# Two graph attention layers: query products of the second layer two steps ahead and in front of the sums, edge products of the first layer three steps ahead

## The chip, the cores and the metric

The kernel runs on one core of one Trainium2 chip. The metric is the device time of one execution in microseconds. Three runs of the kernel before gave 5523.93, 5535.52 and 5536.22 us; their median is 5535.52 us.

## What is computed

Two graph layers, one after the other, over 6250 nodes and 200,000 edges sorted by target node. Each edge reads the row of its source node and the query of its target node, makes a score, and the scores of all edges of one target go through a softmax; the output of a node is the weighted sum of its edges' rows. Cut to what matters:

```
# layer 0 (4 heads of 32), e = projected edge attributes
kj    = k[src] + e
alpha = sum_c(q[dst] * kj) / sqrt(32)
a     = softmax of alpha over the edges of one dst
out   = segment_sum((v[src] + e) * a, dst)
# layer 1 (one head of 256)
s     = sum_c(q[dst] * k[src]) / 16 + edge_weight * we + be
a     = softmax of s over the edges of one dst
out   = segment_sum(v[src] * a, dst)
```

Around each edge stage there are small dense stages over the nodes (projections, a gate, layer norms, a feed-forward net), which the change doesn't touch.

## The kernel before

**Tiles, steps and chunks.** The edges are cut into tiles of 512 (4 groups of 128). A tile is paired with a window of 128 target nodes, 440 pairs in all; one pair is a *step*. Eight steps (st = 0 to 7) make a *chunk*; 55 chunks per layer. The same function edge(L) is written for each engine and run for L0 and for L1; chunks() calls its emit with `scores` (make the scores of chunk c) and `sums` (weigh and sum the messages of chunk c - 1), so each chunk scores its own edges while it sums the one before. There are 54 transitions between chunks with scores per layer.

**One step.** POOL issues four indirect DMAs (line 582), which gather 512 source rows of 1 KB into SBUF. It may run ahead: it waits only for the scores of the step five before (LEAD), for the landing of the gathers two steps before (`gathered`), and for a buffer that was freed long ago. SP loads for each pair the targets (`dst_row`, broadcast, 256 KB, line 431), the queries of the window (`qw`, 96 or 192.8 KB, line 433) and in layer 0 the edge attributes (`ea`, 128 KB, line 436), into four places; the load of pair g + 2 waits until the query products of pair g - 2 are counted on the semaphore `q`. A one-hot matrix `oht` (targets against nodes) is made by ACT in layer 0 (lines 668, 672) and by DVE in layer 1 (line 907).

**PE** (all its products have line 1291, the helper mm) makes for a step: in layer 0 the edge products edge_keys (ps<-w_c,ea, 4 matmuls) for DVE's line 916; the query products queries (ps<-qw,oht, 12 matmuls), which bring q[dst] to the edges; in layer 1 also bias_products (ps<-qw,oht with 3 columns, 4 matmuls), which give q times the key bias; and back (ps<-msg,oh or ps<-rows,oh, 4 matmuls), which sums the messages of a tile of the chunk before. PSUM has two buffers of each kind: edge_keys of pair g waits until DVE added those of g - 2 (semaphore `added`), queries of pair g until the scores of g - 2 are made (`score`), back until line 1089 took the sum two before (`acc`) and until the messages are weighed (`msg`).

**DVE** goes in a fixed order through a step. Layer 0: reduce the scores of the step before (line 928), multiply by the query products (line 923), add the edge products of the next step to its gathered rows (line 916), weigh messages (line 1064), accumulate sums (line 1089). Layer 1: dots, which multiplies and sums in one (line 939, four of them), the one-hot of the step after next (line 907), the weighed one-hots `oh` (line 1069), accumulate.

**The transition.** With the scores of a chunk complete, DVE masks them (line 989, semaphore `masked`) and PE transposes them (turn, lines 1370 and 1371). A scan over the edges for the maximum of each target follows in several pieces, which go to and fro between DVE and PE: scan_tiles (lines 999 to 1006), PE's arrange (ps<-spread,sel_h), scan_ends (lines 1012 to 1025), PE's carry_back (ps<-carry,sel_ht), scan_carried (lines 1030 to 1039), PE's turn_back (line 1385), subtract, PE's shrink_first. They lie in steps 0 and 1 of the next chunk, among that chunk's own products.

**What sets the order.** Each engine's order is written out by hand in emit, and an engine works its instructions in that order: a product that waits holds up all behind it. In PE's emit a step from 2 on is

```
if scores and more(c, st + 2):
    edge_keys(c, st + 2)
if scores and more(c, st + 1):
    queries(c, par, st + 1)
    if st + 1 < CH:
        bias_products(par, st + 1)
for r in L.summed[st] if sums and (L is L0 or st < CH - 1) else ():
    back(past, pp, r)
```

Of the kernel before, what the change touches and what calls it, by code (L numbers as in the profile page):

```python
# [31 lines left out]
CH = 8  # L32
# [34 lines left out]
def build(nc, a, out):  # L67
    ctx = ExitStack()
    with ctx:
# [1217 lines left out]
        def _(pe):  # L1287
# [39 lines left out]
            def edge(L):  # L1327
# [16 lines left out]
                def queries(c, par, st):  # L1344
                    c, st = c + st // CH, st % CH
                    g, b = CH * c + st, st % 2
                    after(pe, s["score"], g - 1)
                    queries_ready(c, st)
                    for j in range(JT):
                        for m in range(3):  # L1350
                            i = mm(q_ps(L, b)[:, j * L.D:(j + 1) * L.D], oht[st % PLACES][:, j * P:(j + 1) * P],
                                   qw[st % PLACES][:, m * L.QD:m * L.QD + L.D], m == 0, m == 2)
                    if L is L0 or st == 1:
                        i.then_inc(s["q"], 1)

                def bias_products(par, st):

                    if L is L1:
# [4 lines left out]
                        if st != 1:  # L1363
                            i.then_inc(s["q"], 1)
# [38 lines left out]
                def emit(c, par, scores, sums):  # L1403
                    past, pp = c - 1, 1 - par
                    if not sums:
                        edge_keys(c, 0)
                        edge_keys(c, 1)
                        queries(c, par, 0)
                    if sums:
                        turn(past)  # L1410

                    if scores:
                        bias_products(par, 0)
                    if L is L1 and sums and not (isinstance(past, int) and past == 0):
# [3 lines left out]
                    if scores and L is L1:  # L1418
                        queries_ready(c, 1)
                        bias_products(par, 1)  # L1420
                    if sums:
                        arrange(past)
                    if scores and L is L1:
                        queries(c, par, 1)
                    if sums:
                        carry_back(past)
                    if scores:
                        edge_keys(c, 2)
                        queries(c, par, 2)
                    if sums:  # L1430
                        turn_back(past)
                    if scores:
                        edge_keys(c, 3)
                    if sums:
                        shrink_first(past)
                    if scores:
                        bias_products(par, 2)
                    for st in range(2, CH):
                        if scores and more(c, st + 2):
                            edge_keys(c, st + 2)  # L1440
                        if scores and more(c, st + 1):
                            queries(c, par, st + 1)
                            if st + 1 < CH:
                                bias_products(par, st + 1)
# [143 lines left out]
```

## Time and profile before

| | |
|---|---|
| median of three runs | 5535.52 us (5523.93 to 5536.22) |
| the profiled execution | 5506.24 us |
| its span in the profile | 5504.4 us |
| PE busy | 3896.4 us (71%) |
| DVE busy | 4245.4 us (77%) |
| ACT busy | 1736.3 us (32%) |
| POOL busy | 3779.5 us (69%) |
| edge stage of layer 0, first to last gather | 147.5 to 2452.2 us |
| edge stage of layer 1, first to last gather | 2746.8 to 5115.5 us |
| mean granted clock of TensorE | 0.871 |

A row of the profile names the line, the engine, the operation and the tiles (written <- read). Busy time counts compute instructions; for POOL's gathers it is the time of the issuing instruction, while the transfer itself shows only in who waits for it. "Idle before" is the time that the engine stood still just before such instructions, with what ended it. "issue" there means that the profile shows nothing the engine waited for.

### The profile page before, as it was taken

The page shows a single profiled execution, that of the slowest core. Times are in us where ns is not written, and L with a number is a line of the kernel's source. Part 1 is how long each engine was busy: PE and PEld are TensorE (multiplying, and loading weights), DVE is VectorE, ACT ScalarE, POOL GpSimd, SP SyncE. Part 2 cuts the span into 40 slices and gives each one's busy share as a digit, 9 for nine tenths or more (in the row PEclk, how much of TensorE's full clock was granted, in tenths as well). Part 3 has the DMA queues.
Part 4 walks back from the last instruction along what each step waited for, and adds up shares of the span by engine and source line. Part 5 has one row for each costly group of instructions (what it writes and reads, how often), then busy time and mean ns, then how long its engine had stood idle before and what let it go on. Part 6 is the DMA issues. An engine that isn't in the chain of part 4 may idle for free.

```text
span 5504.4 us, 104662 instructions
## 1 busy us (share of the span) xinstructions
PE 3896.4 (71%) x26899; PEld 3265.3 (59%) x26899; DVE 4245.4 (77%) x14513; ACT 1736.3 (32%) x4325; POOL 3779.5 (69%) x4032
## 2 busy tenths in 40 slices
PE   7566666666666666666667777777777777777898
PEld 3556665656566665664445555555556656555687
DVE  7688778778877878776667777777777777777688
ACT  1466666666666666663300000000000000000132
POOL 0677777777777777762377777777777777777465
PEclk9788888888888888878978898988988888888899
DMA  6787878778888888763477777777777777777222
GB/s 178 201 216 210 208 207 217 206 208 212 216 214 205 214 213 213 209 171 108 119 196 202 196 200 197 197 201 200 200 195 200 202 200 204 198 194 199 78 81 67
DMA packets 777206, 1039.57 MB, mean 189 GB/s; under 512 B 206911, under 2 KB 528272, under 8 KB 776608
## 3 DMA queue, kind: packets, MB, share of 16 engines
q1 hardware_dynamic: 466736, 499.53, 35.0%
q0 software_dynamic: 169040, 436.01, 29.8%
q10 hardware_dynamic: 140832, 97.33, 5.7%
q8 instruction: 219, 3.59, 0.3%
q14 instruction: 379, 3.10, 0.2%
HBM read 929.76 MB, written 128.40 MB: 192 GB/s over the span
## 4 chain that ended last, share of the span: by engine, by line
POOL 28%; issue 28%; DMA 20%; DVE 10%; PE 9%; DVEq 2%; POOLq 1%; ACT 0%; ACTq 0%; SPq 0%
POOL rows L582 27%; DMA rows<-kv_d,idx 9%; PE ps L1291 9%; DMA rows<-x_d,idx 8%; DMA acc_d<-acc 2%; DVE prod L939 2%; DVE oh L1069 1%; DVE acc L1089 1%; DVEq L1145 1%; DVE oht L907 1%; POOL nq L605 1%; DVEq L1147 1%; DMA idx<-idx_d 1%; PE ps L1490 1%; POOLq L604 1%
## 5 line engine op out<-in xcount | busy, mean ns | idle before, releaser
L582 POOL DMA_INDIRECT rows<-kv_d,idx x1760 | 1713.4, 974 | 718.1 <-issue 524.2
L582 POOL DMA_INDIRECT rows<-x_d,idx x1760 | 1778.9, 1011 | 592.8 <-issue 517.7
L1291 PE MATMUL ps<-qw,oht 128*128 128x128 bf16 (+2 forms) x12320 | 1219.8, 252 | 27.1 <-DVE oht L907 26.9
L1291 PEld LDWEIGHTS ps<-qw,oht 128*128 128x128 bf16 x12320 | 1037.0, 106 | 229.3 <-issue 40.2
L1291 PE MATMUL ps<-rows,oh 128*128 128x257 f32 x3520 | 981.4, 433 | 209.9 <-DVE oh L1069 158.5
L939 DVE CUSTOM_DVE_ANT_0 prod<-rows,ps 128x256 f32<-128x256 f32 x1760 | 637.0, 418 | 413.4 <-DMA rows<-x_d,idx 307.6
L1291 PEld LDWEIGHTS ps<-rows,oh 128*128 128x128 f32 x3520 | 723.2, 214 | 339.1 <-DVE oh L1069 224.8
L916 DVE TENSOR_TENSOR rows<-rows,ps 128x1024 f32<-128x1024 f32 x440 | 536.0, 1218 | 355.7 <-DMA rows<-kv_d,idx 340.3
L1291 PE MATMUL ps<-msg,oh 128*128 128x132 f32 x3520 | 556.0, 309 | 347.7 <-DVE msg L1064 186.8
L708 ACT ACTIVATE pen_r<-ps 128x128 f32<-128x128 f32 (+1 forms) x110 | 30.0, 272 | 2188.0 <-PE ps L1371 2179.8
L1291 PEld LDWEIGHTS ps<-msg,oh 128*128 128x128 f32 x3520 | 484.1, 211 | 392.8 <-DVE msg L1064 374.6
L1291 PE MATMUL ps<-w_c,ea 128*128 128x128 f32 x3520 | 592.8, 323 | 30.4 <-DMA ea<-in_eaT 24.5
L1291 PEld LDWEIGHTS ps<-w_c,ea 128*128 128x128 f32 x3520 | 542.5, 235 | 40.1 <-issue 23.7
L678 ACT ACTIVATE oh<-iota_row,rel 128x128 f32<-128x128 f32 x1760 | 542.0, 386 | 33.3 <-PE ps L1291 32.0
L1069 DVE TENSOR_SCALAR oh<-iota_row,rel,prob 128x128 f32<-128x128 f32 x1760 | 489.9, 362 | 1.1 <-issue 0.7
L668 ACT ACTIVATE oht<-dst_row,node_tab 128x512 bf16<-128x512 int32 x440 | 312.0, 710 | 147.5 <-DMA dst_row<-in_dst_row 115.4
L1089 DVE SCALAR_TENSOR_TENSOR acc<-acc,keep_tab,ps 128x132 f32<-128x132 f32 (+1 forms) x770 | 317.6, 412 | 49.1 <-issue 26.2
L928 DVE TENSOR_REDUCE score<-prod 128x16 f32<-128x512 f32 x440 | 301.8, 686 | 44.7 <-issue 11.1
L672 ACT ACTIVATE oht<-oht,ones 128x512 bf16<-128x512 bf16 x440 | 311.4, 720 | 27.2 <-issue 1.1
L923 DVE TENSOR_TENSOR prod<-rows,ps 128x512 f32<-128x512 f32 x440 | 298.6, 679 | 15.6 <-PE ps L1291 7.6
L1064 DVE TENSOR_TENSOR msg<-rows,prob 128x512 f32<-128x512 f32 x440 | 292.4, 685 | 0.9 <-issue 0.6
L595 POOL TENSOR_TENSOR rows<-rows,minus_half 128x1 f32<-128x1 f32 x196 | 106.4, 558 | 252.9 <-DVE rows L1166 252.9
(205 smaller groups left out, 4341.2 us busy)
## 6 DMA issues: line engine op xcount, KB each, us to landing
dst_row<-in_dst_row SPq DMA_DIRECT2D x880, 256.0 KB
qw<-q_d SPq DMA_DIRECT2D x440, 192.8 KB
acc_d<-acc ACTq DMA_DIRECT2D x440, 128.5 KB
ea<-in_eaT SPq DMA_DIRECT2D x440, 128.0 KB
qw<-q_d SPq DMA_DIRECT2D x440, 96.0 KB
acc_d<-acc ACTq DMA_DIRECT2D x440, 66.0 KB
rows<-kv_d,idx POOLq DMA_INDIRECT x1760
rows<-x_d,idx POOLq DMA_INDIRECT x1760
```

Source lines behind the costliest of these rows:

```text
L582: pool.indirect_dma_start(out=L.rows[par][:, st, j, 0:D], out_offset=None, in_=L.table, in_offset=bass.IndirectOffsetOnAxis(ap=idx[par][:, ...
L668: act.activation(oht[st % PLACES][:, :], dst_row[st % PLACES][:, :], ACT.Abs, scale=-1.0, bias=node_tab[:, bass.ds(g, 1)])
L672: act.activation(oht[st % PLACES][:, :], oht[st % PLACES][:, :], ACT.Relu, scale=-1.0, bias=ones[:, 0:1])\
L678: act.activation(oh[:, st % OHS, j, :], iota_row[:, :], ACT.Abs, scale=-1.0, bias=rel[par][:, st, j:j + 1])
L916: v.tensor_tensor(kv, kv, e_ps(b).rearrange("p (j n) -> p j n", j=JT).unsqueeze(2) .to_broadcast([P, JT, 2, DM]), ALU.add).then_inc(s["add ...
L923: v.tensor_tensor(half, kv_rows[par][:, st, :, 0:DM], q_ps(L, st % 2).rearrange("p (j n) -> p j n", j=JT), ALU.mult)
L928: v.tensor_reduce(score[par][:, st * JT:(st + 1) * JT, :], prod[:, :, st % 2 * DM:(st % 2 + 1) * DM] .rearrange("p j (h n) -> p j h n", h= ...
L939: i = v.tensor_tensor_reduce(out=prod[:, j, :], in0=x1_rows[par][:, st, j, 0:D], in1=q_ps(L, b)[:, j * D:(j + 1) * D], scale=1.0, scalar=0 ...
L1064: v.tensor_tensor(m, kv_rows[par][:, st, :, DM:2 * DM].rearrange("p j (h c) -> p j h c", h=HEADS), prob[par][:, st * JT:(st + 1) * JT, :]. ...
L1069: i = v.tensor_scalar(oh[:, st % OHS, j, :], iota_row[:, :], rel[par][:, st, j:j + 1], prob[par][:, st * JT + j, 0:1], ALU.is_equal, ALU.mult)
L1089: v.scalar_tensor_tensor(acc[st % ACCS][:, 0:L.AW], old[:, 0:L.AW], keep_tab[:, bass.ds(g, 1)], agg_ps(L, b), ALU.mult, ALU.add).then_inc( ...
L1291: return pe.matmul(out_, lhsT=lhsT, rhs=rhs, start=first, stop=last)
```

## The change

Only PE's instructions move; DVE, ACT, POOL and SP keep theirs.

- Layer 1: queries of step st + 2, no longer of st + 1, are made in step st. So the products of steps 0 and 1 of a chunk are made in steps 6 and 7 of the chunk before, those of step 2 stand in the transition where those of step 1 stood, those of step 3 in front of turn_back.
- Layer 1: the bias products of steps 0 and 1 both stand right behind turn, those of steps 2 and 3 both behind shrink_first. The count on `q` now always comes with a step's bias products; before, step 1's came with its query products.
- Layer 0: edge_keys of step st + 3, no longer of st + 2, are made in step st, and stand behind the queries, no longer in front of them. In the transition edge_keys of steps 3 and 4 stand where those of 2 and 3 stood.

```diff
-                    if L is L0 or st == 1:
+                    if L is L0:
                         i.then_inc(s["q"], 1)
...
-                        if st != 1:
-                            i.then_inc(s["q"], 1)
+                        i.then_inc(s["q"], 1)
...
                         queries(c, par, 0)
+                        if L is L1:
+                            queries(c, par, 1)
                     if sums:
                         turn(past)
-
                     if scores:
                         bias_products(par, 0)
+                        bias_products(par, 1)
                     if L is L1 and sums and not (isinstance(past, int) and past == 0):
                         back(past - 1, par, CH - 1)
                     if scores and L is L0:
                         queries(c, par, 1)
-                    if scores and L is L1:
-                        queries_ready(c, 1)
-                        bias_products(par, 1)
+                        if not sums:
+                            edge_keys(c, 2)
                     if sums:
                         arrange(past)
                     if scores and L is L1:
-                        queries(c, par, 1)
+                        queries(c, par, 2)
                     if sums:
                         carry_back(past)
                     if scores:
-                        edge_keys(c, 2)
-                        queries(c, par, 2)
+                        edge_keys(c, 3)
+                        queries(c, par, 2 if L is L0 else 3)
                     if sums:
                         turn_back(past)
                     if scores:
-                        edge_keys(c, 3)
+                        edge_keys(c, 4)
                     if sums:
                         shrink_first(past)
                     if scores:
                         bias_products(par, 2)
+                        bias_products(par, 3)
                     for st in range(2, CH):
-                        if scores and more(c, st + 2):
-                            edge_keys(c, st + 2)
-                        if scores and more(c, st + 1):
-                            queries(c, par, st + 1)
-                            if st + 1 < CH:
-                                bias_products(par, st + 1)
+                        ahead = st + (1 if L is L0 else 2)
+                        if scores and more(c, ahead):
+                            queries(c, par, ahead)
+                            if ahead < CH:
+                                bias_products(par, ahead)
+                        if scores and more(c, st + 3):
+                            edge_keys(c, st + 3)
```

On PE at the transition between two chunks of layer 0 there stood before, from step 6 on (the numbers behind ea, qw and oht are the place, which is the step modulo 4; lines 1370 and 1371 are turn, ps<-msg,oh is back, carry is carry_back):

```order
L1291 MATMUL ps<-w_c,ea0 128x128 x4
L1291 MATMUL ps<-qw3,oht3 128x128 x12
L1291 MATMUL ps<-msg,oh 128x132 x4
L1291 MATMUL ps<-w_c,ea1 128x128 x4
L1291 MATMUL ps<-qw0,oht0 128x128 x12
L1291 MATMUL ps<-msg,oh 128x132 x4
L1370 MATMUL ps<-ident,biased 128x128
L1371 MATMUL ps<-ident,pen 128x128
L1291 MATMUL ps<-qw1,oht1 128x128 x12
L1291 MATMUL ps<-spread,sel_h4 4x128
L1291 MATMUL ps<-carry,sel_ht4 128x64
L1291 MATMUL ps<-w_c,ea2 128x128 x4
```

and after the change, from step 6 on too (turn has lines 1369 and 1370):

```order
L1291 MATMUL ps<-qw3,oht3 128x128 x12
L1291 MATMUL ps<-w_c,ea1 128x128 x4
L1291 MATMUL ps<-msg,oh 128x132 x4
L1291 MATMUL ps<-qw0,oht0 128x128 x12
L1291 MATMUL ps<-w_c,ea2 128x128 x4
L1291 MATMUL ps<-msg,oh 128x132 x4
L1369 MATMUL ps<-ident,biased 128x128
L1370 MATMUL ps<-ident,pen 128x128
L1291 MATMUL ps<-qw1,oht1 128x128 x12
L1291 MATMUL ps<-spread,sel_h4 4x128
L1291 MATMUL ps<-carry,sel_ht4 128x64
L1291 MATMUL ps<-w_c,ea3 128x128 x4
```

The edge products that read ea2, those of step 2 of the new chunk, moved from behind carry_back to a place ahead of the last back and of turn.

On PE at the transition of layer 1 there stood before, from step 6 on (128x256 are the query products, 128x3 the bias products, ps<-rows0,oh is back):

```order
L1291 MATMUL ps<-rows0,oh 128x257 x8
L1291 MATMUL ps<-qw0,oht0 128x256 x12
L1370 MATMUL ps<-ident,biased 32x128
L1371 MATMUL ps<-ident,pen 32x128
L1291 MATMUL ps<-qw0,oht0 128x3 x4
L1291 MATMUL ps<-rows0,oh 128x257 x4
L1291 MATMUL ps<-qw1,oht1 128x3 x4
L1291 MATMUL ps<-spread,sel_h1 1x128
L1291 MATMUL ps<-qw1,oht1 128x256 x12
L1291 MATMUL ps<-carry,sel_ht1 32x64
L1291 MATMUL ps<-qw2,oht2 128x256 x12
L1385 MATMUL ps<-ident,full 128x32
```

and after the change:

```order
L1291 MATMUL ps<-rows1,oh 128x257 x8
L1291 MATMUL ps<-qw1,oht1 128x256 x12
L1369 MATMUL ps<-ident,biased 32x128
L1370 MATMUL ps<-ident,pen 32x128
L1291 MATMUL ps<-qw0,oht0 128x3 x4
L1291 MATMUL ps<-qw1,oht1 128x3 x4
L1291 MATMUL ps<-rows1,oh 128x257 x4
L1291 MATMUL ps<-spread,sel_h1 1x128
L1291 MATMUL ps<-qw2,oht2 128x256 x12
L1291 MATMUL ps<-carry,sel_ht1 32x64
L1291 MATMUL ps<-qw3,oht3 128x256 x12
L1384 MATMUL ps<-ident,full 128x32
```

As many products stand between turn and turn_back as before, but each is of the next step, and the bias products of step 1, which are now counted on `q`, stand right behind those of step 0.

## Rows read from the trace of the kernel before

**Rows 1.** The page: busy time, and the chain by engine and line
```profile
PE 3896.4 (71%) x26899; PEld 3265.3 (59%) x26899; DVE 4245.4 (77%) x14513; ACT 1736.3 (32%) x4325; POOL 3779.5 (69%) x4032
POOL 28%; issue 28%; DMA 20%; DVE 10%; PE 9%; DVEq 2%; POOLq 1%; ACT 0%; ACTq 0%; SPq 0%
```
**Rows 2.** The gathers' line: ns min/median/max, first and last start; then all idle before them
```profile
L582 POOL DMA_INDIRECT rows<-kv_d,idx x1760: 940/946/1630, 147.5 to 2452.2; - x196
L582 POOL DMA_INDIRECT rows<-x_d,idx x1760: 992/998/1257, 2746.8 to 5115.5; - x196
...
L582 POOL DMA_INDIRECT rows<-kv_d,idx x1760 | 1713.4, 974 | 718.1 <-issue 524.2
L582 POOL DMA_INDIRECT rows<-x_d,idx x1760 | 1778.9, 1011 | 592.8 <-issue 517.7
```
**Rows 3.** Timeline, POOL's longest waits of layer 1, four in a row
```profile
3586.72 1.09 POOL L582 DMA_INDIRECT rows<-x_d,idx  x1 [2.38 <-issue]
3753.78 1.00 POOL L582 DMA_INDIRECT rows<-x_d,idx  x1 [3.54 <-issue]
3920.94 0.99 POOL L582 DMA_INDIRECT rows<-x_d,idx  x1 [1.86 <-issue]
4089.41 1.00 POOL L582 DMA_INDIRECT rows<-x_d,idx  x1 [4.04 <-issue]
```
**Rows 4.** Who waited for whom in 200 to 2462 us: total us, times, longest
```profile
DVE rows L916 <- DMA rows<-kv_d,idx: 327.0, 208, 5.3
POOL rows L582 <- DMA rows<-kv_d,idx: 59.8, 109, 2.1
POOL rows L582 <- DVE score L928: 6.1, 20, 0.3
DVE prod L923 <- PE ps L1291: 4.8, 9, 0.8
```
**Rows 5.** The same view in 2796 to 5122 us
```profile
DVE prod L939 <- DMA rows<-x_d,idx: 280.7, 201, 6.2
DVE prod L939 <- PE ps L1291: 72.4, 79, 2.2
POOL rows L582 <- DMA rows<-x_d,idx: 38.6, 94, 1.5
POOL rows L582 <- DVE score L939: 8.8, 29, 0.3
```
**Rows 6.** Timeline of a layer 0 transition, PE and DVE: start, us, row, idle before
```profile
2246.05 1.05 PE L1291 MATMUL ps<-w_c,ea 128*128 128x128 f32 x8
2247.61 1.12 PE L1291 MATMUL ps<-msg,oh 128*128 128x132 f32 x8
2248.65 1.22 DVE L916 TENSOR_TENSOR rows<-rows,ps 128x1024 f32<-128x1024 f32 x1
2250.34 0.33 PE L1370 MATMUL ps<-ident,biased 128*128 128x128 f32 x1 [1.61 <-DVEq L990]
2255.75 1.22 DVE L916 TENSOR_TENSOR rows<-rows,ps 128x1024 f32<-128x1024 f32 x1 [2.81 <-DMA rows<-kv_d,idx]
```
**Rows 7.** Timeline of a layer 1 transition: turn, carry_back, turn_back and SP's target loads
```profile
3054.35 0.40 PE L1370 MATMUL ps<-ident,biased 128*32 128x128 f32 x1 [4.11 <-DVEq L990]
3055.87 0.33 SPq L431 DMA_DIRECT2D dst_row<-in_dst_row  x1
3061.21 1.49 PE L1291 MATMUL ps<-qw,oht 128*128 128x256 bf16 x12
3061.83 0.33 SPq L431 DMA_DIRECT2D dst_row<-in_dst_row  x1
3064.63 0.24 PE L1385 MATMUL ps<-ident,full 32*128 32x32 f32 x1 [1.93 <-DVEq L1039]
```
**Rows 8.** Stretches of that transition: PE, PEld, DVE, ACT, POOL, clock, DMA share, GB/s
```profile
3060.00:3063.00 3.00, 2.70 (x24) 1.89 (x21) 2.54 (x15) 0.00 (x0) 2.38 (x3) 1.00 0.92 277
```

## The prediction

> **What bounds the kernel now.** I read the page first, for busy shares. No engine is near full: DVE has 77%, PE 71%, POOL 69%, and the chain that ended last names POOL and "issue" for 56% [rows 1]. That pair made me look at POOL's line. The reader should see there that POOL is not idle for 31% of the time in any useful sense. A gather's instruction takes 0.946 us in layer 0 and 0.998 in layer 1 in the median [rows 2], and between two of them lie 0.30 us in which POOL waits for nothing that shows. So 1760 gathers need at least 1760 x 1.246 = 2193 us in layer 0 and 1760 x 1.298 = 2284 us in layer 1. The stages take, from first gather to the end of the last, 2305.7 and 2369.7 us [rows 2]. POOL's own pace fills 95% and 96% of them, and the two stages are 85% of the span. Nothing that PE does shortens that pace.
>
> What is left over is 2305.7 - 2193 = 113 us and 2369.7 - 2284 = 86 us. A part is longer gather instructions: 1713.4 - 1760 x 0.946 = 48 us and 1778.9 - 1760 x 0.998 = 22 us [rows 2]. The rest, some 64 us in each layer, is waiting. I asked what POOL waited for. Its longest waits come every 167 to 168 us [rows 3], which is 128 gathers at 1.30 us; they follow POOL's count of instructions and are no one's fault on PE. Then there are waits for the landing of the gathers two steps before: 59.8 us in 109 times in layer 0 and 38.6 us in 94 times in layer 1 [rows 4, 5]. Of each the usual 0.30 us would pass anyway, which leaves 27 and 10 us. Never did POOL wait for DVE's scores: the rows that name them have 0.3 us as their longest [rows 4, 5], the usual gap. DVE, in turn, waited for gathers for 327.0 us in layer 0 and 280.7 us in layer 1 [rows 4, 5], that is 6.0 and 5.2 us per chunk (by 54 of them). So the order is: POOL's pace, then landings, then DVE with slack, then PE behind DVE.
>
> **The change part by part.** It adds and takes away no instruction; it moves PE's products.
>
> *Layer 1, query products two steps ahead.* They were late for DVE: line 939 waited for PE for 72.4 us in 79 times [rows 5], mostly in the steps 0 to 2 of a chunk. Those 72.4 us should go nearly to zero, since the products of steps 0 and 1 are now made while the old chunk runs out. But DVE then comes earlier to a gather that hasn't landed, and the 280.7 us grow by as much. Cover: POOL's pace. Worth on the path: 0. The products put in front of turn run while PE stood idle 4.11 us before turn [rows 7], and take 1.49 us [rows 7], so turn isn't late.
>
> *Layer 1, step 3's products in front of turn_back.* The 12 matmuls begin when DVE has made the scores of step 1, and PE stood idle for 1.93 us before turn_back [rows 7]. I take 0.3 us of delay of the scan per transition, 54 x 0.3 = 16 us on DVE, between 0 (the idle time holds them) and 1.49 us (it doesn't). DVE's 5.2 us of waiting for gathers per chunk hide either. Worth: 0.
>
> *Layer 0, edge products behind the queries and one step earlier.* In steps 2 to 6 they fill the time in which PE waits for DVE to weigh messages, and DVE needs nothing of PE there (4.8 us in all [rows 4]). Worth: 0. In step 7 the move costs something. The edge products of the new chunk's step 2 may start only when DVE has added those of step 0, and DVE does that after its last work for the old chunk. The last back and turn now queue behind that. In the timeline DVE's add begins at 2248.65 and ends at 2249.87; the edge products take 1.05 us, back 1.12 us, so turn can start at 2252.04 instead of 2250.34 [rows 6]. With back's sum and the transposed scores both later, DVE's scan begins some 1.7 us later: 54 x 1.7 = 92 us on DVE. What covers it is seen in the same rows: DVE reaches the add of the next step and waits 2.81 us for the gather. Over the layer it is 6.0 us of such waiting per chunk against 1.7. And if a chunk has less, POOL doesn't ask for a score until five steps later. Worth: 0; without the cover, 92 us.
>
> *Loads.* SP's four places are freed by the count on `q`, so moving it moves DMAs, and this is the one way in which PE touches POOL. In layer 1 the count for steps 0 and 1 now comes at once, behind turn. Before, SP loaded at 3055.87 behind turn and again at 3061.83, 6 us apart [rows 7]; now the second load (256 + 192.8 KB) follows the first within some 1.5 us. The counts of steps 2 and 3 come together too, and the counts of steps 4 to 7 a step earlier, so before turn there is a longer stretch with no loads. At the rate of this transition, 277 GB/s [rows 8], 449 KB are 1.6 us. A gather in flight then lands up to 1.6 us later and one that used to meet the second load lands earlier. The change in all lies between 0 - 10 us (all waits of layer 1 for landings go) and 54 x 1.6 = 86 us (none of the delay is hidden). Landing ended POOL's wait in 94 of 440 steps, and cost 10 us in them, so the lower end is the nearer. For two of eight steps getting worse and one better I take +3 us. In layer 0 the load that is tied to step 1's queries was issued later than its count anyway, and the rest moves by about one edge product: 0, within +-10 us of landing waits.
>
> Here a rule bears on the load term. The Trainium skill, page "DMA: Bandwidth & Descriptors", section "Queues, rings and completion order", says that each DMA engine takes turns between queues packet by packet; by it a second load in SP's queue stands behind the first and not ahead of the gather, and the sum would stay at 0. The same section says that a semaphore increment lands only after earlier writes of that DMA engine on all queues, which speaks the other way, for a late landing. No row of the kernel before tells which weighs more.
>
> Sum on the profiled execution: 5506 + 0 + 0 + 0 + 3 = 5509 us. The median of the runs is 29 us above that execution, so I forecast 5538 us, no change that can be measured. About 0.3%, 17 us, is what a measurement of this kernel can tell from no change.
>
> **The rivals.**
>
> *A. Bunched loads make POOL wait (slower).* At each transition of layer 1 the two loads, and the stores of sums that ACT issues behind turn, meet the gather of step 1, and POOL's gather of step 3 waits for its landing. It decides when landings of step 1 come later than POOL's next step allows in most chunks rather than in one of five. For: landings already end one of five waits, and the DMA share is 0.92 there [rows 8]. Against: the bytes are the same, and the stretch before has fewer loads. Price: 54 x 1.6 us x 0.4 (between the one in five of today and the half) = +35 us: 5570. Chance 0.20.
>
> *B. The late turn of layer 0 shows (slower).* If DVE were paced by its scan and not by gathers, 92 us would come through: 5628. Against it stand 6.0 us of waiting per chunk. Chance 0.04.
>
> *C. Landing waits shrink (faster).* In layer 1 loads are asked for a step earlier through most of the chunk and in both layers PE asks sooner, so fewer loads fall beside a gather that POOL is about to need. It can win at most the 27 + 10 us of landing waits and what long gather instructions cost through contention; I price it at two thirds of 37 us, -25: 5510. Chance 0.14.
>
> *D. DVE was the pace after all (faster).* Then the 72.4 us that line 939 waited for PE come off: 5463. The chain does spend 19% on DVE and PE [rows 1]. Against: DVE never ended a wait of POOL, and the waits of DVE for gathers are four times as long. Chance 0.04.
>
> *That the change doesn't do what it says* can be left out for layer 1: the order rows show the products moved. For layer 0 it is half true: in steps 2 to 6 the edge products only change places with the sums and the queries, since DVE's add, which lets them start, lies where it lay.
>
> **How the numbers follow.** No change (A to D absent) has 0.58. Faster by over 0.3% is C and D, 0.18; slower is A and B, 0.24. The range goes from 5505 (C, a little over its price) to 5580 (A, with a part of the 86 us bound); outside lie B, D and the far ends of A and C, in all under 2 in 10.
>
> **What would show it.** In the profile after: the first and last gather of both layers within some 10 us of their old distance; gathers' medians 0.95 and 1.00 us; no POOL wait for scores above 0.3 us. Line 939's wait for PE in layer 1 should fall from 72.4 us to under 15, and its wait for gathers rise from 280.7 to about 340. In layer 0 the wait of line 916 for gathers should fall from 327.0 by 50 to 92 us, to 235 to 280, as turn is some 1.7 us later. SP's two loads behind turn should be 1 to 2 us apart. POOL's wait for landings in layer 1 decides between the forecast (up to 45 us) and A (70 us and more). I am wrong if the gather stages shorten or lengthen by over 17 us together: then landings or DVE hold POOL in a way that I read as covered.

## The result and the profile after

The changed kernel takes 5578.08 us in the median of four runs (5575.36 to 5592.18), the kernel before 5533.41 us (5523.93 to 5536.22). The ratio is 1.0089, with a 95% interval of 1.0068 to 1.011: slower by 0.9%, 45 us. The forecast was no change, 5538 us. The profiled execution of the kernel before was 27 us faster than its median and that of the changed one 14 us slower than its own, so the two traces are 86 us apart where the medians are 45 us apart. To keep this out, the changed kernel was run again (e5_changed), and readings are checked against that second trace.

The gathers' own line in the changed kernel: ns min/median/max, and first and last start. Its first and last starts answer to the upper rows of [rows 2].

```profile
L582 POOL DMA_INDIRECT rows<-kv_d,idx x1760: 940/946/1698, 148.0 to 2467.8; - x196
...
L582 POOL DMA_INDIRECT rows<-x_d,idx x1760: 992/998/1257, 2774.5 to 5199.7; - x196
```

The pace of a gather is untouched: 946 and 998 ns. From the first to the last start layer 1's gathers took 2368.7 us before and now take 2425.2 us, 56 us more. Layer 0's went from 2304.7 to 2319.8 us, 15 us more; but in e6_l1_only and e18_l1_only_held below, whose layer 0 is that of the kernel before, it is 2324.9 and 2321.0 us, so these 15 us are not the change's: the trace of the kernel before was short there.

What POOL and DVE waited for in layer 1 of the changed kernel, in 2824 to 5208 us (total us, times, longest), against [rows 5]:

```profile
PE ps L1291 <- DVE oht L907: 501.1, 296, 4.8
DVE prod L939 <- DMA rows<-x_d,idx: 286.9, 181, 4.7
POOL rows L582 <- DMA rows<-x_d,idx: 76.8, 88, 3.1
DVE prod L939 <- PE ps L1291: 43.4, 52, 1.0
POOL rows L582 <- PE ps L1291: 23.9, 45, 1.5
POOL rows L582 <- DVE score L939: 12.8, 42, 0.3
```

POOL's wait for landings has doubled, from 38.6 to 76.8 us, in fewer cases, so each is longer. It still never waits for a score: 0.3 us is the longest. DVE waits less for PE (72.4 to 43.4 us, and none over 1.0 us), which is what the change was to do, and as long for gathers as before. PE has now a wait that it hardly had (26.9 us in the whole span before): its products, a step further ahead, wait 501.1 us for one-hots that DVE has not made yet. That costs nothing on this kind of chip, as e7_l1_held below shows. The row that puts 23.9 us of POOL's waits down to PE needs care: POOL waits for several semaphores at once, the sums of PE among them are those of two chunks before, and 12 of its 15 waits of over 0.6 us stand at step 1, where landings are late (below).

The same view for layer 0, 200 to 2478 us, against [rows 4]:

```profile
PE ps L1291 <- DMA ea<-in_eaT: 273.0, 54, 7.0
DVE acc L1089 <- PE ps L1291: 257.8, 55, 6.6
DVE rows L916 <- DMA rows<-kv_d,idx: 73.2, 149, 3.9
POOL rows L582 <- DMA rows<-kv_d,idx: 58.2, 106, 2.1
POOL rows L582 <- DVE score L928: 18.6, 61, 0.3
```

Once in each of 54 transitions PE waits some 5 us for `ea`. DVE's wait for gathers has shrunk from 327.0 to 73.2 us. POOL's is what it was (59.8 to 58.2 us).

One transition of layer 0 in the changed kernel, PE, DVE and SP's loads of `ea`, against [rows 6]:

```profile
2263.36 0.33 SPq L418 DMA_DIRECT2D idx_d<-idx  x1
2265.56 0.48 SPq L436 DMA_DIRECT2D ea<-in_eaT  x1
2267.87 0.47 SPq L436 DMA_DIRECT2D ea<-in_eaT  x1
2267.98 1.22 DVE L916 TENSOR_TENSOR rows<-rows,ps 128x1024 f32<-128x1024 f32 x1
2270.86 2.05 PE L1291 MATMUL ps<-w_c,ea 128*128 128x128 f32 x8 [4.41 <-DMA ea<-in_eaT]
2272.70 1.97 PE L1291 MATMUL ps<-msg,oh 128*128 128x132 f32 x8
2274.46 0.42 PE L1369 MATMUL ps<-ident,biased 128*128 128x128 f32 x1
```

DVE's add ends at 2269.20, but the edge products that stand before back and turn begin at 2270.86, because their `ea` has not landed: SP issues that load only behind keep_idx (line 418, at 2263.36), which waits until DVE has marked the chunk's edges with their owners (line 976). Then they run at half the pace of [rows 6], 2.05 us against 1.05, after the long stop (the clock is in the last section). Turn is at 2274.46, 5.3 us after the add ended; in [rows 6] it was 0.5 us.

And one transition of layer 1 in the changed kernel (turn, SP's loads of targets, ACT's stores, POOL):

```profile
4101.56 0.30 PE L1369 MATMUL ps<-ident,biased 128*32 128x128 f32 x1 [1.85 <-DVEq L990]
4102.06 4.85 ACTq L694 DMA_DIRECT2D acc_d<-acc  x3
4102.11 1.01 POOL L582 DMA_INDIRECT rows<-x_d,idx  x1 [0.30 <-issue]
4102.87 0.33 SPq L431 DMA_DIRECT2D dst_row<-in_dst_row  x1
4105.36 0.34 SPq L431 DMA_DIRECT2D dst_row<-in_dst_row  x1
4111.25 1.00 POOL L582 DMA_INDIRECT rows<-x_d,idx  x1 [0.30 <-issue]
4114.28 1.00 POOL L582 DMA_INDIRECT rows<-x_d,idx  x1 [2.04 <-DMA rows<-x_d,idx]
```

The two loads come at 4102.87 and 4105.36, 2.5 us apart and no longer 6 us [rows 7]. POOL issues the gathers of step 2 from 4102.11 on, right among them and ACT's three stores. Its first gather of step 4, at 4114.28, waits 2.04 us for them to land. The prediction's rival A had named the gather of step 1 and the wait at step 3; it is step 2 and step 4.

### The profile page after: what moved, and what is told of

Same layout as the page of the kernel before. It is cut to its first block, busy times and chain, and to the rows that moved or that the text cites. A ratio compares the mean times of both kernels' runs of the same rounds, so it can differ in the third digit from the quotient of the medians.

```text
span 5590.3 us, 104607 instructions
## 1 busy us (share of the span) xinstructions
PE 3998.9 (72%) x26899; PEld 3287.0 (59%) x26899; DVE 4256.0 (76%) x14513; ACT 1722.8 (31%) x4325; POOL 3790.7 (68%) x4032
## 3 DMA queue, kind: packets, MB, share of 16 engines
q0 software_dynamic: 169040, 436.01, 30.3%
## 4 chain that ended last, share of the span: by engine, by line
issue 26%; POOL 24%; DMA 23%; PE 11%; DVE 9%; DVEq 2%; ACT 2%; POOLq 1%; ACTq 1%; SPq 0%
POOL rows L582 23%; DMA rows<-x_d,idx 12%; PE ps L1291 10%; DMA rows<-kv_d,idx 8%; DMA acc_d<-acc 2%; DVE rows L916 1%; DVE prod L939 1%; DMA ea<-in_eaT 1%; ACT oh L678 1%; POOL nq L605 1%; DVE acc L1089 1%; DVEq L1147 1%; PE ps L1492 1%; DVE oht L907 1%; POOLq L604 1%
## 5 line engine op out<-in xcount | busy, mean ns | idle before, releaser
L1291 PE MATMUL ps<-qw,oht 128*128 128x128 bf16 (+2 forms) x12320 | 1273.8, 259 | 545.7 <-DVE oht L907 531.6
L1291 PEld LDWEIGHTS ps<-qw,oht 128*128 128x128 bf16 x12320 | 1016.7, 107 | 806.7 <-DVE score L939 602.8
L1291 PE MATMUL ps<-w_c,ea 128*128 128x128 f32 x3520 | 650.7, 342 | 512.4 <-DMA ea<-in_eaT 303.1
L1291 PE MATMUL ps<-rows,oh 128*128 128x257 f32 x3520 | 934.9, 417 | 2.4 <-DVE oh L1069 2.3
L1291 PEld LDWEIGHTS ps<-w_c,ea 128*128 128x128 f32 x3520 | 555.9, 241 | 582.9 <-issue 293.7
L1291 PEld LDWEIGHTS ps<-rows,oh 128*128 128x128 f32 x3520 | 707.8, 209 | 109.1 <-DVE oh L1069 3.3
L1291 PE MATMUL ps<-msg,oh 128*128 128x132 f32 x3520 | 521.2, 302 | 8.8 <-DVE msg L1064 4.7
```

The source lines that it names most:

```text
L1291: return pe.matmul(out_, lhsT=lhsT, rhs=rhs, start=first, stop=last)
```

## The experiments

Each kernel was timed in five rounds beside the kernel before on the same chip; the ratio is to that. The chips are of two kinds. On two draws the kernel before took 5533.38 and 5520.90 us, as in the first measurement (below: *chips of kind 1*); on three it took 7033.54, 6955.53 and 6956.38 us (*kind 2*). A ratio is good for its own kind of chip only; one chip of kind 2 was drawn twice and gave 7033.54 and then 6955.53 us, so times are compared within a set. The changed kernel as it is ran on kind 1 only, e10_scores_held and e11_before_held, with their repetitions, on kind 2 only.

| run | kernel | median us | kernel before | ratio, 95% interval |
|---|---|---|---|---|
| e1_l1_only | layer 1's part | 6988.44 | 7033.54 | 0.9936 (0.9916 to 0.9956) |
| e2_l0_only | layer 0's part | 7164.74 | 7033.54 | 1.0179 (1.0158 to 1.0199) |
| e3_border | changed, border of layer 0 restored | 7014.43 | 7033.54 | 0.9975 (0.9959 to 0.9992) |
| e4_l1_held | changed, all loads of layer 1 held | 7190.68 | 7033.54 | 1.0196 (1.0167 to 1.0224) |
| e5_changed | changed | 5584.16 | 5533.38 | 1.0093 (1.008 to 1.0106) |
| e6_l1_only | layer 1's part | 5573.06 | 5533.38 | 1.0072 (1.0059 to 1.0085) |
| e7_l1_held | changed, all loads of layer 1 held | 5524.32 | 5533.38 | 0.9984 (0.9973 to 0.9996) |
| e8_border | as e3_border | 5580.64 | 5533.38 | 1.0081 (1.0064 to 1.0098) |
| e9_second_held | changed, second load held | 7027.57 | 6955.53 | 1.011 (1.0079 to 1.014) |
| e10_scores_held | changed, loads held by scores | 7009.07 | 6955.53 | 1.0077 (1.0054 to 1.01) |
| e11_before_held | before, all loads held | 6938.55 | 6955.53 | 0.9974 (0.996 to 0.9987) |
| e12_l1_only_held | layer 1's part, all loads held | 6924.6 | 6955.53 | 0.9956 (0.9939 to 0.9974) |
| e13_second_held | as e9 | 7034.05 | 6956.38 | 1.0106 (1.0082 to 1.0129) |
| e14_scores_held | as e10 | 7016.7 | 6956.38 | 1.0078 (1.0059 to 1.0098) |
| e15_before_held | as e11 | 6953.18 | 6956.38 | 0.9989 (0.9968 to 1.0009) |
| e16_l1_only_held | as e12 | 6932.28 | 6956.38 | 0.9959 (0.9944 to 0.9975) |
| e17_second_held | as e9 | 5541.2 | 5520.9 | 1.0035 (1.0024 to 1.0046) |
| e18_l1_only_held | as e12 | 5517.54 | 5520.9 | 0.9989 (0.9977 to 1.0002) |

**First set, a chip of kind 2.** e1_l1_only takes layer 0's edits back, e2_l0_only layer 1's. In e3_border only the border is taken back:

```diff
                         queries(c, par, 1)
-                        if not sums:
-                            edge_keys(c, 2)
+                        edge_keys(c, 2)
...
-                        if scores and more(c, st + 3):
+                        if scores and st != CH - 1 and more(c, st + 3):
                             edge_keys(c, st + 3)
```

e4_l1_held leaves PE alone and edits SP in load_ahead:

```diff
                     wait(s["q"], g - 1)
+                    if L is L1:
+                        wait(s["score"], g - 2)
+                        if st == 3:
+                            wait(s["spreadback"], c)
                     load_pair(
```

> The change in layer 1 alone; layer 0 keeps its order of before. Theory (two separate costs: in layer 0 the edge products of the next chunk's step 2 wait for the load of ea and hold back and turn; in layer 1 the loads of targets and queries fall at other times and gathers land later): slower than before by 20 to 50 us, POOL's stage of layer 1 (2746.8 to 5115.5 us before, 2774.5 to 5199.7 in the changed kernel) longer by 20 to 56 us, layer 0 as before (line 916's wait for gathers about 327 us). Rival (the whole loss is layer 0's, and layer 1's longer stage in the one profile is chance): within 10 us of before. Rival (layer 1's part is a gain that layer 0 eats): faster than before by 10 us or more.

> The change in layer 0 alone; layer 1 keeps its order of before. Theory: slower than before by 10 to 30 us: PE waits some 5 us per transition for ea (273.0 us in 54 times in the changed kernel), line 916's wait for gathers falls to about 75 us, POOL's stage of layer 0 grows by some 15 us and the way from its last gather to layer 1's first by some 12 us. Rival (all of layer 0's delay is covered by POOL's pace): within 10 us of before.

> The changed kernel, but in layer 0 the edge products of the next chunk's step 2 stand behind queries of step 1, and no longer in front of the last back and of turn; all else as changed. Theory: PE's wait for ea before turn goes (273 us to under 60), turn comes 4 to 6 us earlier against POOL's steps, line 916's wait for gathers goes back above 250 us, and the kernel is 10 to 30 us faster than the changed one. Rival (layer 0 costs nothing): as slow as the changed kernel, within 8 us.

> The changed kernel, with PE's order untouched, but in layer 1 SP holds each load of a pair until the scores of the step three before the loading step's pair are made, and the second load behind turn until carry_back, so about when they came before the change. Theory (load times make gathers land late in layer 1): 15 to 50 us faster than the changed kernel, POOL's wait for landings in layer 1 from 76.8 us back to about 40. Rival (it is PE's order itself: products in front of the sums make sums and so DVE late): no faster than the changed kernel, landings' wait still above 65 us.

Measured: layer 1's part alone is faster by 0.6%, layer 0's alone slower by 1.8%, with the border restored the change is faster by 0.25%, and with layer 1's loads held it is slower by 2.0%. That layer 1's part would be a gain was one of e1's rivals; layer 0's loss is 131 us where 10 to 30 were expected, and holding the loads brought nothing that was hoped for. This chip is bound elsewhere. The waits of e2_l0_only over the whole span:

```profile
PE ps L1291 <- issue: 803.0, 728, 7.3
POOL rows L582 <- DVE score L928: 944.2, 197, 9.1
POOL rows L582 <- DVE score L939: 635.9, 180, 9.4
```

Here PE stands still for 803 us with nothing in the profile that it waits for, up to 7.3 us at a time, and POOL waits for DVE's scores for 1580 us, up to 9.4 us at a time. The gathers' instructions take what they took. So POOL no longer sets the pace; it follows DVE's scores, and what delays PE and DVE can reach the time: layer 0's part costs 1.8%, query products made earlier gain 0.6%. Nearly all of layer 0's loss is the border: from first to last start its gathers take 3129.6 us in e1_l1_only (layer 0 as before), 3278.8 us in e2_l0_only and 3144.3 us in e3_border. It is not the load of `ea` there (7.1 us of waiting in 200 to 3436 us of e2_l0_only), but DVE's add, for which PE's products wait 429.5 us in 119 times. Why PE stops on such a chip isn't shown by any run.

**Second set, a chip of kind 1.** e7_l1_held is e4_l1_held with the same waits written on one line.

> The changed kernel itself, beside the kernel before on the same chip, since another chip ran the kernel before in 7033.54 us and not in 5533. If this chip is like the first: slower than before by 0.7 to 1.1%. If it is like the second, where layer 0's part alone cost 1.8% and layer 1's alone gained 0.6%: slower by 1.0 to 1.4%, the two parts added.

> Layer 1's part alone, as e1_l1_only, on this chip. On a chip like the first: slower than before by 0.2 to 0.9% if load times in layer 1 make gathers land late (POOL's wait for landings in layer 1 near 77 us); within 0.2% of before if the first chip's loss was all layer 0's. On a chip like the second: faster by 0.4 to 0.9%, because DVE there doesn't wait for gathers and query products made earlier are of use.

> The changed kernel with layer 1's loads held as in e4_l1_held. On a chip like the first: 0.2 to 0.8% faster than the changed kernel if load times are the cost in layer 1, no faster if PE's order is. On a chip like the second: slower than the changed kernel by some 0.8%, since there the loads are late already.

> The changed kernel with layer 0's edge products of the next step 2 moved back behind queries of step 1, as e3_border. On a chip like the first: 0.2 to 0.5% faster than the changed kernel, PE's wait for ea in layer 0 from 273 us to under 60, line 916's wait for gathers above 250 us. On a chip like the second: 1.2 to 1.7% faster than the changed kernel.

Measured: the changed kernel 1.0093, as in the first measurement. Layer 1's part alone has 1.0072, so most of the loss. Restoring layer 0's border does what it should in the trace and nothing for the time. Waits in e8_border, 200 to 2470 us:

```profile
DVE rows L916 <- DMA rows<-kv_d,idx: 348.2, 222, 6.7
POOL rows L582 <- DMA rows<-kv_d,idx: 65.0, 115, 2.1
PE ps L1291 <- DMA ea<-in_eaT: 48.1, 41, 2.4
```

The wait for `ea` is down from 261.1 us in e5_changed to 48.1, DVE waits for gathers as long as before the change, and the time is 3.5 us less, within the intervals. The expectation of 0.2 to 0.5% failed. Holding the loads, with PE's order untouched, makes the kernel 59.8 us faster than the changed one: 5584.16 to 5524.32, or 1.1%, more than the 0.2 to 0.8% expected. The line of the gathers (busy, mean ns, idle before and its releasers), in e5_changed and in e7_l1_held:

```profile
L582 POOL DMA_INDIRECT rows<-x_d,idx x1760 | 1778.0, 1010 | 645.0 <-issue 516.0 <-DMA rows<-x_d,idx 80.9 <-PE ps L1291 22.3
```
```profile
L582 POOL DMA_INDIRECT rows<-x_d,idx x1760 | 1778.2, 1010 | 597.7 <-issue 520.7 <-DMA rows<-x_d,idx 37.3 <-DMA idx<-idx_d 19.6
```

POOL's wait for landings goes from 80.9 to 37.3 us, where the kernel before had 38.6. Its stage, first to last start, goes from 2419.7 to 2372.7 us (2368.7 before the change). These 47 us are the whole difference between the two profiled executions (5572.6 and 5526.34 us); the medians are 60 us apart, since the profiled one of e5_changed was the fastest of its five. PE's new wait for one-hots stays (461.9 us in e7_l1_held in 2824 to 5208 us), so it was not the cost. A transition of e7_l1_held, the same things as shown above for the changed kernel:

```profile
4061.95 0.30 PE L1369 MATMUL ps<-ident,biased 128*32 128x128 f32 x1 [0.68 <-DVEq L990]
4063.25 0.33 SPq L431 DMA_DIRECT2D dst_row<-in_dst_row  x1
4069.45 0.42 PE L1291 MATMUL ps<-carry,sel_ht 1*32 1x64 f32 x2
4070.72 0.33 SPq L431 DMA_DIRECT2D dst_row<-in_dst_row  x1
4073.41 0.99 POOL L582 DMA_INDIRECT rows<-x_d,idx  x1 [0.30 <-issue]
```

The second load is back at 7.5 us behind the first, and POOL's first gather of step 4 (4073.41) doesn't wait.

**Third and fourth set, chips of kind 2.** Which of the two holds does it? e9_second_held has only the wait on spreadback for the second load, e10_scores_held only the wait on score. e11_before_held puts both holds into the kernel before, e12_l1_only_held into layer 1's part.

> The changed kernel; of the holds of e7_l1_held only one: SP's load for step 5, the second behind turn, waits for carry_back. Theory A (the bunch of two loads behind turn is what delays the gather of step 2, whose landing POOL's step 4 waits for): most of the 60 us come back, 35 us or more faster than the changed kernel (5584 us), POOL's wait for landings in layer 1 from 80 us to under 55, its waits before step 4 from 46 us in the gaps to some 15. Theory B (it is the loads that come a step earlier all over the chunk): within 15 us of the changed kernel. On a chip where the kernel before takes 7000 us neither is tested.

> The changed kernel; of the holds of e7_l1_held the other one: each load of layer 1 waits for the scores of the pair three before the pair of SP's step, and the two loads behind turn stay together. Theory A: up to 25 us faster than the changed kernel only, waits before POOL's step 4 still near 40 us. Theory B: 40 us or more faster. The two runs need not add up to 60 us exactly if a landing is late for both causes.

> The kernel before, with the same holds on layer 1's loads as e7_l1_held. There the loads come about then anyway. If e7_l1_held beats the kernel before by 0.16% because of PE's order, this one is within 0.15% of the kernel before. If the holds themselves put loads at better times than the kernel before had, this one is faster than the kernel before by 0.15% or more.

> Layer 1's part of the change with the holds, layer 0 as before the change. If layer 0's part costs what lies between e5_changed and e6_l1_only (11 us), this is 5 to 15 us faster than e7_l1_held (5524 us), and so the fastest, 0.25 to 0.45% under the kernel before. If layer 0's part costs nothing: within 5 us of e7_l1_held.

These fell on a chip of kind 2, and so did their repetition:

> As e9_second_held. On a chip like the first: theory A (the two loads together behind turn): 35 us or more faster than the changed kernel's 5584 us, POOL's wait for landings in layer 1 under 55 us; theory B (all loads a step earlier): within 15 us of 5584.

> As e10_scores_held. On a chip like the first: theory A: up to 25 us under 5584 us; theory B: 40 us or more under it.

> As e11_before_held. On a chip like the first: within 0.15% of the kernel before if the kernel before already had its loads at these times; faster by more if the holds put them better.

> As e12_l1_only_held. On a chip like the first: 5 to 15 us faster than e7_l1_held (5524 us) if layer 0's part costs 11 us, within 5 us of it if it costs nothing.

They tell nothing of landings. For kind 2 they agree with each other: with layer 0's part and one of the holds in, 1.1% and 0.8% slower (both holds, in e4_l1_held: 2.0%); without layer 0's part 0.4% faster (0.9956 and 0.9959). The changed kernel as it is was not run on such a chip, so what a hold does to it there isn't known. The kernel before with holds had 0.9974 and 0.9989, the second not clear of 1. On kind 1 it wasn't run: whether the 9 us by which e7_l1_held beats the kernel before come from PE's order or from the holds stays open.

**Fifth set, kind 1 again.**

> As e9_second_held and e13_second_held. On a chip like the first: theory A (two loads together behind turn): 35 us or more under the changed kernel's 5584 us, POOL's wait for landings in layer 1 under 55 us; theory B (all loads a step earlier): within 15 us of 5584. On a chip like the other two: slower than the kernel before by 1.1%, as twice before.

> As e12_l1_only_held. On a chip like the first: 5 to 15 us faster than e7_l1_held (5524 us) if layer 0's part costs 11 us, within 5 us of it if it costs nothing. On a chip like the other two: 0.4% faster than the kernel before, as twice before.

Holding the second load alone gives 1.0035, against 1.0093 of the changed kernel: 0.58%, 32 us. That is neither the 35 us or more of theory A nor the 15 us or less of theory B, though near to A; POOL's wait for landings, 49.0 us, is under A's 55. The other hold brings it from 1.0035 to 0.9984, 0.51%, 28 us. Both steps go from one chip of kind 1 to another, so the split is less sure than the sum, and the scores hold alone was not run on kind 1. The timeline tells the two causes apart. Counted there are the steps of POOL in layer 1 (chunks 1 to 54, one first gather each) that began over 0.6 us after the step before ended:

| POOL's step | before | e5_changed | e17_second_held | e7_l1_held |
|---|---|---|---|---|
| 4 | 10 | 39 | 9 | 11 |
| 0 and 1 | 9 | 24 | 28 | 9 |
| 2, 3, 5, 6, 7 | 24 | 25 | 18 | 24 |

The second load behind turn makes step 4 wait; holding it clears step 4. Steps 0 and 1 wait too, and only with the hold by scores, which undoes the loads that come a step earlier, is that gone. Beyond the usual 0.30 us the waits counted at step 4 are 10.5, 46.5, 10.8 and 12.3 us in the four traces, those at steps 0 and 1 are 11.0, 25.3, 30.3 and 12.9 us. A landing ended 33 of the 39 waits at step 4 in e5_changed, and 5 of the 10 before. So in the traces the bunch costs 36 us and the earlier loads 14 to 17 us: the first is the larger. (Of the 28 us between e17_second_held and e7_l1_held layer 1's stage shows 16.6, from 2389.3 to 2372.7 us; another 10.7 lie in layer 0's, which the holds don't touch.)

The traces also have the time at which the last increment of `gathered` came. Here is how long after the end of a step's fourth gather instruction its rows had landed, in the median, in us. POOL waits for them after the four gathers of the next step, which take 4 x 1.30 = 5.2 us:

| gathers of step | before | e5_changed | e17_second_held | e7_l1_held |
|---|---|---|---|---|
| 2 (step 4 waits for them) | 4.3 | 5.5 | 4.2 | 4.1 |
| 6 (step 0 waits) | 3.1 | 4.0 | 4.3 | 3.2 |
| 7 (step 1 waits) | 4.0 | 4.9 | 4.7 | 4.0 |

SP's load of targets for step 5 begins 5.3, 2.2, 6.6 and 6.5 us behind that for step 4 in these four (medians). The other loads: while POOL stood in steps 0 and 1, 74, 16, 13 and 58 of them began; in steps 4 to 6, 193, 254, 259 and 224. Of step 7 this doesn't hold (61, 53, 53 and 56), so which load delays its gathers isn't shown. The waits of POOL in e17_second_held in 2824 to 5208 us:

```profile
POOL rows L582 <- DMA rows<-x_d,idx: 49.0, 84, 2.4
POOL rows L582 <- PE ps L1291: 22.7, 41, 2.6
```

lie between the changed kernel's 79.7 us (e5_changed in the same stretch) and e7_l1_held's 37.0.

e18_l1_only_held has 0.9989, e7_l1_held, which has layer 0's part too, 0.9984: no difference beyond the intervals, and not the 5 to 15 us expected if layer 0's part cost 11 us. So on chips of kind 1 layer 0's part costs nothing that can be measured; the 11 us between e5_changed and e6_l1_only are within overlapping intervals. The version of e12, e16 and e18 is the one that is slower on neither kind: 0.4% faster than the kernel before on kind 2, level with it on kind 1 (0.9977 to 1.0002). On kind 2 e1_l1_only, without holds, did as well (0.9936, intervals overlap), but it is 0.7% slower on kind 1.

## Why the prediction was right or wrong

**What bounds the kernel: right on chips of kind 1.** POOL's pace stayed at 946 and 998 ns, POOL never waited over 0.3 us for a score, and what PE and DVE lost or gained did not reach the time. One reading was wrong: POOL's long waits come 124 gathers apart and not 128; those of [rows 3] stand before gathers 624, 748, 872 and 996 of layer 1 (counted from 0). Nothing in the sum hangs on it. On kind 2 the same view reads otherwise; one trace of one chip couldn't show that.

**"Layer 1, query products two steps ahead": worth 0, right.** Line 939's wait for PE was to fall under 15 us and fell to 43.4, in waits of up to 1.0 us that remain. Its wait for gathers was to rise to 340 us; it is 286.9 (233.0 in e7_l1_held), and why it didn't rise isn't shown. With the loads held the time is that of the kernel before or a little under it (0.9984).

**"Layer 0 ... in step 7 the move costs something": 0 on the path, right; its size on DVE wrong.** I gave turn 1.7 us of delay and line 916's wait for gathers a fall to 235 to 280 us. The wait fell to 73.2 us, by 254 us or 4.7 us per transition. I had counted the wait for DVE's add and the two groups of matmuls, and not the load of `ea` that the moved products read: SP has that load behind keep_idx. What frees a load was followed for `q` and not for `ea`. Turn came 4.8 us later in the transition shown (5.3 us behind the add and not 0.5), not 1.7. The cover was 6.0 us per chunk, so it just held. e8_border and e18_l1_only_held show that nothing of it that can be measured reached the time on kind 1, so the 0 was right with less to spare than I thought. Rival B's price of 92 us is too low by this delay (54 x 4.8 = 259 us). Its condition, that DVE is not paced by gathers, is what chips of kind 2 have; layer 0's part cost 131 us there in e2_l0_only, by waits for DVE's add and not for `ea`.

**"Loads": the step that failed.** I saw the mechanism, bounded it between -10 and +86 us and took +3, because landings ended a wait in only 94 of 440 steps. The measured term is 60 us by the medians of e5_changed and e7_l1_held, and 47 us by their profiled executions. Two things were wrong in it. First, the average over 440 steps was the wrong row to be near to. The touched steps are not average: the gathers of step 2, which now meet two loads and ACT's three stores, already landed latest of all before the change (4.3 us, against 2.6 to 4.0 us for the others), and 5.2 us is where POOL begins to wait. Landing 1.2 us later, they cross that line in most chunks: 39 waits of 54 where there were 10. The delay itself was bounded rightly, at 1.6 us; what I took as hidden wasn't. Second, I took the loads that come a step earlier for neutral, or in rival C for a gain. They cost 14 to 17 us in the traces (28 us by the ratios): the gathers of steps 6 and 7 land 0.9 us later, and POOL's steps 0 and 1 wait for them. Transfers that have slack (the loads are needed two steps later) delay one that has none.

**The rule of the Trainium skill.** By the Trainium skill, "DMA: Bandwidth & Descriptors", section "Queues, rings and completion order", taking turns between queues would have kept the sum at 0; the semaphore that lands only after earlier writes of a DMA engine on all queues speaks for late landings. The trace agrees with late landings: POOL's wait for them is 76.8 us, not 38.6, and step 2's gathers land 5.5 us after their last instruction, not 4.3. Whether it is that ordering or plain sharing of bandwidth no run here tells.

**The rivals.** A is what happened, one step later than I wrote it and as the larger part of the loss: the bunch at the turn was priced at +35 us and measures 32 by the ratios, 36 by the waits before step 4. I gave it 0.20. That its price came so near is in part luck: 1.6 us in 40% of the transitions was assumed, and 39 of 54, or 72%, wait, 1.2 us each on average beyond the usual gap. C went the other way. D is excluded on kind 1. The forecast was no change; the measured 5578.08 us is 40 us above it, and inside the range (5505 to 5580) only just.

**What would show it.** The test named for A, a landing wait of POOL of 70 us or more in layer 1, came out as A: 76.8 us. The two loads are 2.5 us apart in the transition shown and 2.2 us in the median, not 1 to 2. The gather stages lengthened by 72 us together (56 in layer 1, and in layer 0 the 15 that are not the change's), well over the 17 us that I had named as the sign of being wrong.

## What to carry to other kernels

When an engine's order moves, look at every semaphore count that moves with it and at the DMAs that wait for it: on chips of kind 1 all of the loss came through loads that were released earlier, while the compute that was moved cost and gained next to nothing. A load with slack should not be released as early as its buffer allows if a transfer without slack shares the DMA engines; holding it until it is needed gave back 60 us of 5584. And the cost of a later landing isn't the share of steps that wait today times the delay: look at how far the steps that are touched are from waiting. Last, a change that costs nothing on one chip can cost 1.8% on another that is bound elsewhere: time both versions on the same chip, and say which kind it was.

## What the runs showed of the hardware

The same kernel took 5521 to 5533 us on chips of kind 1 and 6956 to 7034 us on kind 2, some 26 to 27% more, with gathers' instructions of the same length (1767.4 us for 1760 of layer 1 in e15_before_held, 1778.9 before). On kind 2 PE stood still before its products for 766 to 940 us with no releaser in the profile, on kind 1 for under 9 us. The mean granted clock of TensorE was 0.76 to 0.79 there and 0.85 to 0.87 on kind 1; whether that is a cause or comes of PE's stops isn't shown. An edit that was neutral on one kind of chip was 1.8% on the other. POOL's long waits every 167 us, 124 gathers apart [rows 3], are in the trace of e7_l1_held too, at 3435.94, 3604.28, 4105.47 us and so on.

When a landing of gathers ended a wait of over 0.6 us, POOL's next gather began 0.84 us after the last increment of `gathered` in 18 of 21 such waits of layer 1 before the change and in 54 of 61 in e5_changed.

After PE's stop of 4.41 us, from 2266.45 to 2270.86 us of the changed kernel, the edge products took 2.05 us, and 1.05 us in [rows 6]. The granted clock around it (columns: stretch, then PE, PEld, DVE, ACT, POOL busy, clock, DMA share, GB/s):

```profile
2266.00:2268.00 2.00, 0.44 (x8) 0.27 (x5) 1.82 (x6) 0.40 (x1) 1.50 (x2) 1.00 0.90 162
2268.00:2270.00 2.00, 0.00 (x0) 0.00 (x0) 1.79 (x4) 0.00 (x0) 1.59 (x2) 0.74 0.97 315
2270.00:2272.00 2.00, 1.15 (x5) 1.18 (x6) 0.38 (x1) 0.00 (x0) 1.39 (x3) 0.50 1.09 329
2276.00:2278.00 2.00, 0.55 (x5) 0.09 (x2) 1.74 (x7) 1.82 (x3) 1.63 (x2) 1.00 0.67 162
```

It falls from 1.00 while PE idles, is at 0.50, the lower of the two levels, when PE works again, and is back at 1.00 in 2276 to 2278 us. In the kernel before, where PE idled for 2.33 us before 5084.55 and for 3.53 us before 5089.80, it fell only after PE had begun again:

```profile
5086.00:5088.00 2.00, 0.27 (x3) 0.00 (x0) 1.64 (x9) 0.00 (x0) 0.00 (x0) 1.00 0.92 332
5088.00:5090.00 2.00, 0.20 (x1) 0.13 (x1) 1.65 (x7) 0.00 (x0) 0.00 (x0) 1.00 0.20 74
5090.00:5092.00 2.00, 1.48 (x12) 1.13 (x12) 1.22 (x9) 0.46 (x2) 1.51 (x2) 0.72 0.08 18
5092.00:5094.00 2.00, 1.81 (x13) 1.25 (x10) 2.00 (x11) 0.00 (x0) 1.70 (x2) 0.50 0.47 128
```

So the products right behind a stop of some 4 us can take twice their time, and a price taken from a transition without such a stop is too low.
